# One kernel, one change: the TensorE program of the linear attention becomes a hardware loop over pairs of chunks

## The chip, the cores and the metric

The kernel runs on one core of one Trainium2 chip. The metric is device microseconds per execution of the whole program. It is written by hand in Bass: each engine has its own instruction queue, and every dependency between queues is a semaphore wait.

## The reference

A "macaron" layer over 4 sequences of 1,024 tokens with 128 features, in float32: half of a gated ternary FFN, then a block of causal linear attention with 16 heads of 64 and a GELU MLP, then the same half FFN again. What the change touches is the attention:

```python
Q = _phi((x @ Wq).reshape(b, t, H, DH)).transpose(0, 2, 1, 3)   # _phi = elu + 1
K = _phi((x @ Wk).reshape(b, t, H, DH)).transpose(0, 2, 1, 3)
V = (x @ Wv).reshape(b, t, H, DV).transpose(0, 2, 1, 3)
KV = jnp.einsum('bhti,bhtj->bhtij', K, V)
S = jnp.cumsum(KV, axis=2)
z = jnp.cumsum(K, axis=2)
num = jnp.einsum('bhti,bhtij->bhtj', Q, S)
den = jnp.maximum(jnp.einsum('bhti,bhti->bht', Q, z), EPS_DEN)[..., None]
out = (num / den).transpose(0, 2, 1, 3).reshape(b, t, H * DV)
return out @ Wo
```

## The kernel before

The program has five stages: first FFN, attention, MLP, second FFN, with the ends of the stages overlapped. Large products are made of float32r parts: a high and a low part of the data times a high part of the weights, and the high part times the low weights, so three matmuls each.

The attention goes over 32 chunks of 128 tokens, `n = 0..31`. Two chunks make a half tile `hh` (256 tokens, 16 of them), four chunks make a tile `i` of 512 tokens, and eight chunks make a sequence. For each chunk the TensorE queue does, in this order (`attention_pe`, one Python loop written out in full):

- `token_major("K", n, h)`: the key product of the next chunk, 2 x 3 matmuls of 512 columns (L822, the helper `three`).
- `outputs(g)`: for chunk g = n - 1 first the products of the queries with the running states (L886, steps `I`), then those of the masked scores with the values (L898, steps `O`). They are 64 x 64 tiles; in float32 each of them is two matmul instructions.
- `queries(hh + 1, j)`: the query product of the next half tile, two of its four parts in each chunk (L822, 256 columns), alternating with `token_major("V", n, h)` (L822, 512 columns).
- `transposed_keys(n)` and `transposed_outputs(g)`: transposes (L648).
- `state_products(n)` (L913, steps `D`) and `scores(n)` (L869, steps `S`): again 64 x 64 tiles.
- in every odd chunk the output projection `WO` (24 matmuls of 256 columns, L822) and the transposes of the normalised rows `nT` of the half tile after next.

The queries have two buffers `qf`, the normalised input two pairs `ahh`/`ahl`. ScalarE computes exp and relu of K and Q (L1158, L1159), copies V, the transposed keys and the outputs (L1180, L1188, L1228); VectorE combines exp and relu (L1472, `phi`), divides (L1533 to L1538), takes the low part of the outputs (L1562), adds up the states (L1554) and masks the scores (L1526). GpSimd computes reciprocal roots and the residual sum, SyncE loads and stores. PSUM banks 0, 1, 6 and 7 are a ring; banks 2 to 5 belong to outputs and state products.

A sequence's first chunk leaves out the products with the empty state, its last chunk the state product for the second half of the chunk.

The TensorE program exists twice, as `program(2)` and `program(3)` under a branch on a flag computed on the chip (`pe.If`, `pe.Else`); the first of them is what runs here. Except for this branch no engine jumps anywhere.

Of the kernel before, what the change touches and what calls it, by code (L numbers as in the profile page):

```python
# [5 lines left out]
P = 128  # L6
ALU = mybir.AluOpType
ACT = mybir.ActivationFunctionType
F32 = mybir.dt.float32
# [103 lines left out]
def build_kernel(nc, t, out):  # L113
# [37 lines left out]
    with ctx:  # L151
# [65 lines left out]
        with ExitStack() as s:  # L217
            ahh = [sb(s, f"ahh{h}", [P, 2, P + DH], F32R) for h in range(2)]
            ahl = [sb(s, f"ahl{h}", [P, 2, P + DH], F32R) for h in range(2)]
            ahf = sb(s, "ahf", [P, 2, P + DH])  # L220
            axn = sb(s, "axn", [P, Q, D])
# [5 lines left out]
            ayf = sb(s, "ayf", [P, TILE])  # L227
# [3 lines left out]
            qf = [sb(s, "qf0", [P, PR, TILE // 2])]  # L231
            kt_ = [sb(s, f"kt{k}", [P, DA]) for k in range(2)]
            qf.append(sb(s, "qf1", [P, PR, TILE // 2]))
# [64 lines left out]
        for name, names in (("pe_fn", ["T"]), ("pe_f1", [f"{m}" for m in range(KT)]), ("pe_f2", ["y"]), ("pe_fy", ["T"]),  # L298
# [3 lines left out]
            T[name] = Count(sem(name), names)  # L302

# [46 lines left out]
        def attention_plan():  # L350
# [3 lines left out]
            pe, act, dve, pool, phis, jobs, turns = [], [], [], [], [], [], []  # L354
# [20 lines left out]
            def phi(bank, name):  # L375
                phis.append(name)
                job(bank, name, "act", f"r_{name}")
                act.extend([f"e_{name}", f"r_{name}"])

# [9 lines left out]
            def scores(banks, n):  # L389
                for bank, m in zip(banks, "ab"):  # L390
                    job(bank, f"S{n}{m}", "dve", f"am{n}{m}")

            def state_products(n):
                last = n % CB == CB - 1
                for j in range(2):
                    pe.append(f"D{n}.{j}")
                    jobs.append((f"D{n}.{j}", OB[j], "dve", f"sm{n}.{j}"))
                    if not last:
                        jobs.append((f"D{n}.{j}'", OB[j] + 1, "dve", f"ss{n}.{j}"))
                for name in ("sm",) if last else ("sm", "ss"):  # L400
                    dve.extend(f"{name}{n}.{j}" for j in range(2))
                dve.extend(f"am{n}{m}" for m in "ab")

            def stats(i):
                dve.extend([f"st{i}", f"ag{i}", f"ve{i}"])
                pool.append(f"r1_{i}")

            def once(i):
                dve.extend([f"v1_{i}", f"v2_{i}", f"v3_{i}", f"xp{i}"])
                pool.append(f"r2_{i}")  # L410

            stats(0)
            once(0)
            dve.append("xn0")
            for hh in range(2):
                norm(6 + hh, hh)
                split(hh)
            for h in range(2):
                phi(h, f"K0.{h}")
            dve.append("vt")  # L420
            for j in range(4):
                phi(j, f"Q0.{j}")
            dve.extend([*(f"phi_K0.{h}" for h in range(2)), *(f"phi_Q0.{j}" for j in range(4))])
            for h in range(2):
                values(4 + h, 0, h)
            kt((0, 1), 0)
            state_products(0)
            scores((6, 7), 0)
            stats(1)
            for g in range(NC):  # L430
                c, i, n, hh, old = g % Q, g // Q, g + 1, g // 2, g % CB
                more, queries = n < NC, hh + 1 < NHALF
                if more:
                    for h in range(2):
                        phi(turn(), f"K{n}.{h}")
                        dve.append(f"phi_K{n}.{h}")
                else:
                    for m in range(2):
                        tail((1, 0)[m], f"L0.{m}", "act_f1", f"hi{m}", 0)
# [6 lines left out]
                if c == 1 and i + 1 < NT:  # L446
                    dve.append(f"xn{i + 1}")
                for j in range(2):
                    if queries:
                        phi(turn(), f"Q{hh + 1}.{2 * (g % 2) + j}")  # L450
                        dve.append(f"phi_Q{hh + 1}.{2 * (g % 2) + j}")
                    if more:
                        values(turn(), n, j)
                    if c == 0 and i and j == 0:
                        job(turn(), f"yT{i - 1}", "dve", f"y{i - 1}")
                        dve.append(f"y{i - 1}")
                        pool.append(f"ys{i - 1}")
                if n + 1 == NC:
                    tail(turn(), "N0", "act_fn", "hi", 0)
                if more:  # L460
                    kt((turn(), turn()), n)
                else:
                    for m in range(2):
                        tail((6, 7)[m], f"L0.{m + 2}", "act_f1", ("full2", "hi3")[m], 0)
                    for m in range(2):
                        tail((1, 0)[m], f"L1.{m}", "act_f1", f"hi{m}", 1)
                for j in range(2):
                    job(turn() if more else (2, 5)[j], f"OT{g}.{j}", "dve", f"ol{g}.{j}")
                    act.append(f"oh{g}.{j}")
                    dve.append(f"ol{g}.{j}")  # L470
                if n + 1 == NC:
                    tail(turn(), "N1", "act_fn", "hi", 1)
# [1353 lines left out]
```

## Time and profile before

| what | value |
|---|---|
| median of 3 runs | 854.55 us |
| the runs | 852.06 to 859.12 us |
| profiled execution, its own time | 862.1 us |
| its span, first to last instruction | 860.4 us |
| mean granted TensorE clock | 0.992 |

The profile is one execution. "PE" are TensorE's matmuls, "PEld" its weight loads, which overlap the matmuls; each matmul has one weight load, so that two instructions pass through the queue for each matmul shown. "issue" is time in which an engine waited for nothing that the profile shows. DMA queues q8 and q14 are of the kind "instruction": they bring the engines' program code.

### The profile page before, as it was taken

The page shows a single profiled execution, that of the slowest core. Times are in us where ns is not written, and L with a number is a line of the kernel's source. Part 1 is how long each engine was busy: PE and PEld are TensorE (multiplying, and loading weights), DVE is VectorE, ACT ScalarE, POOL GpSimd, SP SyncE. Part 2 cuts the span into 40 slices and gives each one's busy share as a digit, 9 for nine tenths or more (in the row PEclk, how much of TensorE's full clock was granted, in tenths as well). Part 3 has the DMA queues.
Part 4 walks back from the last instruction along what each step waited for, and adds up shares of the span by engine and source line. Part 5 has one row for each costly group of instructions (what it writes and reads, how often), then busy time and mean ns, then how long its engine had stood idle before and what let it go on. Part 6 is the DMA issues. An engine that isn't in the chain of part 4 may idle for free.

```text
span 860.4 us, 26994 instructions
## 1 busy us (share of the span) xinstructions
PE 796.8 (93%) x11458; PEld 674.6 (78%) x11458; DVE 569.7 (66%) x1290; ACT 563.4 (65%) x1024; POOL 364.4 (42%) x292
## 2 busy tenths in 40 slices
PE   1799999998999999999999999999998799999997
PEld 0688888877788888888888788888786678888886
DVE  7665565376867787687787876778798582818220
ACT  3687777767565654646556556565677477777774
POOL 4597979682001001010000101001276497979784
PEclk9999999999999999999999999999999899999999
DMA  7002120201001001010010100201024320201010
GB/s 256 0 26 60 39 66 8 84 3 51 15 3 41 14 3 53 3 42 14 3 52 4 51 3 27 64 3 40 28 65 118 89 61 13 62 12 50 1 50 26
DMA packets 56762, 34.55 MB, mean 40 GB/s; under 512 B 1984, under 2 KB 55232, under 8 KB 56640
## 3 DMA queue, kind: packets, MB, share of 16 engines
q1 hardware_dynamic: 56640, 32.79, 13.2%
q8 instruction: 93, 1.52, 0.8%
q14 instruction: 29, 0.24, 0.1%
HBM read 22.29 MB, written 10.49 MB: 38 GB/s over the span
## 4 chain that ended last, share of the span: by engine, by line
PE 81%; ACT 6%; issue 5%; DVE 4%; POOL 2%; DMA 1%; SPq 0%; DVEq 0%; ACTq 0%; POOLq 0%
PE ps L677 34%; PE ps L822 21%; PE ps L648 9%; PE ps L886 4%; PE ps L913 4%; PE ps L869 4%; PE ps L898 4%; PE ps L740 3%; ACT ee L1158 1%; DVE xnA L1285 1%; ACT junk L1085 1%; ACT full L1123 1%; DMA xlnA<-x_scratch 1%; ACT gate L1047 1%; POOL alA L1662 1%
## 5 line engine op out<-in xcount | busy, mean ns | idle before, releaser
L1766 POOL TENSOR_TENSOR as<-as,power 128x4 f32<-128x4 f32 x16 | 16.7, 1045 | 292.6 <-DVE as L1485 247.9
L1158 ACT ACTIVATE ee<-ps 128x512 f32<-128x512 f32 x128 | 77.8, 608 | 95.5 <-PE ps L822 69.6
L1662 POOL TENSOR_TENSOR alA<-full,ahA 128x512 fp32r<-128x512 f32 x74 | 100.5, 1371 | 41.9 <-DVE ahA L1325 35.7
L1317 DVE SCALAR_TENSOR_TENSOR full<-ps,sc,gate 128x512 f32<-128x512 f32 x64 | 46.6, 747 | 104.2 <-PE ps L677 63.9
L677 PE MATMUL ps<-ahA,wh 128*128 128x512 f32 x288 | 113.5, 394 | 1.0 <-POOL alA L1662 1.0
L677 PE MATMUL ps<-ahB,wh 128*128 128x512 f32 x288 | 113.4, 394 | 0.1
L677 PE MATMUL ps<-alA,wh 128*128 128x512 f32 x288 | 112.2, 390 | 0.0
L677 PE MATMUL ps<-alB,wh 128*128 128x512 f32 x288 | 112.2, 390 | 0.0
L1662 POOL TENSOR_TENSOR alB<-full,ahB 128x512 fp32r<-128x512 f32 x76 | 99.1, 1318 | 13.0 <-ACT ahB L1066 7.3
L1065 ACT ACTIVATE full<-ps,sc 128x512 f32<-128x512 f32 x86 | 59.5, 692 | 33.3 <-PE ps L677 23.2
L1159 ACT ACTIVATE rr<-ps 128x512 f32<-128x512 f32 x128 | 78.0, 609 | 0.0
L677 PEld LDWEIGHTS ps<-ahA,wh 128*128 128x128 f32 x288 | 54.1, 188 | 13.2 <-POOL alA L1662 2.3
L677 PEld LDWEIGHTS ps<-ahB,wh 128*128 128x128 f32 x288 | 54.1, 188 | 11.4 <-POOL alB L1662 0.6
L677 PEld LDWEIGHTS ps<-alA,wh 128*128 128x128 f32 x288 | 54.1, 188 | 10.9
L677 PEld LDWEIGHTS ps<-alB,wh 128*128 128x128 f32 x288 | 54.1, 188 | 10.8
L1472 DVE SCALAR_TENSOR_TENSOR qf<-ee,rr 128x512 f32<-128x512 f32 x64 | 49.3, 775 | 19.0 <-ACT rr L1159 18.9
L1562 DVE TENSOR_TENSOR ol<-ps,oh 128x512 fp32r<-128x512 f32 x64 | 41.2, 686 | 31.0 <-ACT oh L1228 31.0
L822 PE MATMUL ps<-wah,ahh 128*128 128x512 f32 x128 | 54.5, 426 | 0.3 <-DVE state L1554 0.3
L1243 ACT COPY ayf<-ps 128x256 f32<-128x256 f32 x16 | 6.0, 374 | 73.5 <-PE ps L822 73.5
L869 PE MATMUL ps<-qf,kf 64*64 64x64 f32 x2048 | 39.3, 221 | 13.6 <-issue 13.6
L822 PE MATMUL ps<-wah,ahl 128*128 128x512 f32 x128 | 51.5, 402 | 0.1
L822 PE MATMUL ps<-wal,ahh 128*128 128x512 f32 x128 | 51.2, 400 | 0.0
(179 smaller groups left out, 2248.1 us busy)
## 6 DMA issues: line engine op xcount, KB each, us to landing
wst<-in_ternary SPq DMA_DIRECT2D x5, 512.0 KB, 8.1
stage<-in_attn SPq DMA_DIRECT2D x4, 512.0 KB, 4.6
xlnA<-x_scratch SPq DMA_DIRECT2D x8, 256.0 KB, 2.8
axr<-x_scratch SPq DMA_DIRECT2D x8, 256.0 KB, 4.2
yx_scratch<-ay SPq DMA_DIRECT2D x8, 256.0 KB, 2.3
xs_scratch<-axs SPq DMA_DIRECT2D x8, 256.0 KB, 3.3
xlnA<-yx_scratch SPq DMA_DIRECT2D x8, 256.0 KB, 2.9
xlnB<-yx_scratch SPq DMA_DIRECT2D x8, 256.0 KB, 3.3
```

The source lines that it names most:

```text
L648: ins = nc.tensor.transpose(dst[:, k * P:(k + 1) * P], src, ident[:, :])
L677: ins = nc.tensor.matmul(b[:, :], w[:, col(k):col(k) + P], x_[:, k, :], start=(k == 0 and j == 0), stop=(k == ks[-1] and j == terms - 1))
L822: ins = nc.tensor.matmul(b, w, m, start=(n == 0), stop=(n == len(parts) - 1))
L869: ins = nc.tensor.matmul(banks[m][place, p * DH:(p + 1) * DH], kf[rows, p, place], qf[half][rows, p, tok:tok + DH], start=True, stop=True)
L886: ins = nc.tensor.matmul(banks[j][m][tok, place[p]], qf[(g // 2) % 2][rows, p, first:first + DH], (middle if half else state[k])[rows, p, ...
L1065: nc.scalar.activation(fullh[k % NH][:, :], src, ACT.Gelu, scale=s_).then_inc(*T[f"act_{h}{U}"].step(f"full{m}"))
L1158: nc.scalar.activation(ee[k][:, :], src[:, :], ACT.Exp).then_inc(*X["act"].step(f"e_{name}"))
L1159: nc.scalar.activation(rr[k][:, :], src[:, :], ACT.Relu).then_inc(*X["act"].step(f"r_{name}"))
L1317: nc.vector.scalar_tensor_tensor(fulll[m][:, :], ps[f["bank"]["L1", U, m, "v", n]][:, :], sc[:, KT + m:KT + m + 1], gate[k % NS][:, :], AL ...
L1472: nc.vector.scalar_tensor_tensor(dst, e_, 1.0, r_, ALU.min, ALU.add)\
L1562: nc.vector.tensor_tensor(ol[:, 4 * j:4 * j + 4, own], ps[X["banks"].bank[f"OT{g}.{j}"]][:, :].rearrange("p (k n) -> p k n", n=P), oh[:, 4 ...
L1662: return nc.gpsimd.tensor_tensor(dst, src, hi.bitcast(F32), ALU.subtract)
```

## The change

The TensorE program of the attention is written as `pair(hh)`, two chunks. `pair(0)` and `last_pair(15)` are written out; pairs 1 to 14 are one hardware loop, `pe.Fori(1, NHALF - 1)`, whose body stands once in the code. Only TensorE's queue has the loop; the other queues stay written out in full. For the body to be the same for every pair:

- a wait inside the loop compares a semaphore with a value computed in a register, loop counter times the steps of one pair plus a constant (`hold`). In `outputs`, `state_products` and `scores` a wait on a constant that always holds is put before it.
- the semaphore counts of the work that recurs with a tile and not with a pair (statistics, reciprocal roots, residual) move to semaphores of their own.
- `qf`, `ahh` and `ahl` become one buffer each.
- all four query products go into the odd chunk of a pair (K, outputs, Q0, Q1, V0, Q2, V1, Q3, ...). Normalisation of the next half tile, the output projection of the pair before and its transposes (now per half tile, 2 instead of 4 at once) go into the even chunk.
- a sequence's first chunk computes the products with a state of zeros (a memset in place of a sum on VectorE), its last chunk the state product that was left out.

The core of the diff:

```diff
@@ waits on the TensorE queue
+            rolled, small = [], []
+            def hold(sem, value, per):
+                if rolled:
+                    value = pe.to_reg(rolled[0] * per + (value - per))
+                    if small:
+                        pe.wait_ge(X["pe"].sem, X["pe"].base)
+                pe.wait_ge(sem, value)
+            def after(eng, name):
+                hold(*X[eng].done(name, 0), X["pair"][eng])
             def bank(name):
-                X["banks"].wait_empty(pe, name, 0)
+                if name in X["banks"].prior:
+                    steps, by, _ = X["banks"].prior[name]
+                    hold(*steps.done(by, 0), sum(X["pair"][e] for e in ENG if steps is X[e]))
                 return ps[X["banks"].bank[name]]
@@ outputs
-                        for half, tok in halves if old else halves[1:]:
+                        for half, tok in halves:
@@ state_products
-                both = n % CB < CB - 1
+                both = n + 1 < NC
@@ the TensorE queue
+            def pair(hh):
+                e, o = 2 * hh, 2 * hh + 1
+                for h in range(2):
+                    token_major("K", o, h)
+                outputs(e)
+                norm(hh + 1)
+                for h in range(2):
+                    token_major("V", o, h)
+                if hh:
+                    output_projection(hh - 1)
+                transposed_keys(o)
+                if hh:
+                    back(hh - 1)
+                transposed_outputs(e)
+                state_products(o)
+                scores(o)
+                for h in range(2):
+                    token_major("K", o + 1, h)
+                outputs(o)
+                queries(hh + 1, 0)
+                queries(hh + 1, 1)
+                token_major("V", o + 1, 0)
+                queries(hh + 1, 2)
+                token_major("V", o + 1, 1)
+                queries(hh + 1, 3)
+                transposed_keys(o + 1)
+                transposed_outputs(o)
+                state_products(o + 1)
+                scores(o + 1)
...
+                pair(0)
+                with pe.Fori(1, NHALF - 1) as i:
+                    rolled.append(i)
+                    pair(1)
+                    rolled.pop()
+                X["pe"].next += (NHALF - 3) * X["pair"]["pe"]
+                last_pair(NHALF - 1)
@@ VectorE, phi
-                    if n >= 2 and j == 0:
-                        after("pe", f"O{2 * n - 3}.1")
+                    if n and j == 0:
+                        after("pe", f"I{2 * n - 1}.1")
@@ VectorE, accumulated
-                        if half or old:
+                        if half and n % CB == CB - 1:
+                            ins = nc.vector.memset(after_[:, pairs, :], 0.0)
+                        else:
                             ins = nc.vector.tensor_tensor(after_[:, pairs, :], src, before_[:, pairs, :], ALU.add)
-                        else:
-                            ins = nc.vector.tensor_copy(after_[:, pairs, :], src)
```

## Rows read from the trace of the kernel before

**Rows 1.** The page: busy time by engine, instruction queues, share of the chain that ended last
```profile
PE 796.8 (93%) x11458; PEld 674.6 (78%) x11458; DVE 569.7 (66%) x1290; ACT 563.4 (65%) x1024; POOL 364.4 (42%) x292
...
q8 instruction: 93, 1.52, 0.8%
...
PE 81%; ACT 6%; issue 5%; DVE 4%; POOL 2%; DMA 1%; SPq 0%; DVEq 0%; ACTq 0%; POOLq 0%
```

**Rows 2.** Windows: the attention; busy us and count by engine, granted clock, DMA share, GB/s
```profile
205.00:617.00 412.00, 389.40 (x9491) 344.89 (x9489) 313.71 (x768) 243.37 (x491) 27.05 (x25) 0.99 0.09 26
```

**Rows 3.** Waits of PE, 230 to 617 us: total us, times, longest us
```profile
PE ps L869 <- issue: 13.6, 9, 2.0
PE ps L648 <- DVE xnA L1285: 1.8, 1, 1.8
PE ps L822 <- DVE ol L1562: 1.5, 1, 1.5
PE ps L822 <- DVE state L1554: 1.2, 1, 1.2
PE ps L886 <- issue: 1.1, 2, 0.5
```

**Rows 4.** The chain in order of time around one issue stall: start us, us, what
```profile
258.35 1.09 PE ps L913 x64
259.44 0.48 PE ps L869 x30
259.92 1.52 issue
261.44 0.69 PE ps L869 x29
```

**Rows 5.** DMA of 256 to 261.5 us, 40 slices of 0.1375 us
```profile
GB/s 0 0 0 0 60 0 0 0 0 0 0 0 0 0 0 0 0 0 0 119 0 0 0 0 0 0 0 0 0 0 0 0 0 0 0 0 0 0 0 0
...
q8 instruction: 1, 0.02, 1.5%
```

**Rows 6.** TensorE's timeline, state products and scores without a stall between them
```profile
247.10 1.16 PE L913 MATMUL ps<-vt,kt 64*64 64x65 f32 x64
248.08 1.11 PE L869 MATMUL ps<-qf,kf 64*64 64x64 f32 x64
249.12 0.50 PE L822 MATMUL ps<-wah,ahh 128*128 128x512 f32 x1
```

**Rows 7.** The program's end: last PE matmuls; DMA of 859.9 to 861 us (slices 0.0275 us)
```profile
855.51 0.63 PE L648 MATMUL ps<-ident,yfB 128*128 128x128 f32 x4 [0.88 <-DVE xoA L1291]
...
GB/s 0 0 0 0 0 0 0 0 596 0 0 0 0 0 0 0 0 0 0 0 0 0 0 0 0 0 0 0 0 0 0 0 0 0 0 0 0 0 0 0
```

**Rows 8.** DMA of 856.4 to 858 us, 40 slices of 0.04 us
```profile
GB/s 269 294 307 282 269 691 256 294 256 256 294 269 282 282 282 282 269 282 256 218 141 52 26 0 0 0 0 0 0 0 0 0 0 0 26 102 218 282 282 320
...
q8 instruction: 1, 0.02, 4.6%
```

**Rows 9.** The chain: two long stalls and the key product after each, then an undisturbed one
```profile
325.90 2.00 issue
...
328.86 2.77 PE ps L822 x6
...
380.64 1.88 issue
...
382.86 1.59 PE ps L822 x6
...
343.90 1.40 PE ps L822 x6
```

**Rows 10.** Windows of key product plus outputs: undisturbed, after the stalls of 325.9 and 482.3 us
```profile
238.60:242.30 3.70, 3.70 (x138) 3.09 (x136) 2.00 (x4) 3.13 (x7) 0.00 (x0) 1.00 0.02 4
...
328.80:333.65 4.85, 4.85 (x136) 3.83 (x135) 4.18 (x13) 2.17 (x4) 1.04 (x1) 0.73 0.16 46
...
484.80:490.00 5.20, 5.20 (x139) 4.09 (x135) 4.42 (x13) 2.17 (x4) 1.04 (x1) 0.67 0.21 55
```

**Rows 11.** Lines of VectorE, 205 to 617 us: the shortest instruction and the query combination
```profile
L1472 DVE SCALAR_TENSOR_TENSOR qf<-ee,rr 128x512 f32<-128x512 f32 x64 | 49.3, 775 | 19.0 <-ACT rr L1159 18.9
...
L1481 DVE MEMSET spare<- 128x1 f32 x7 | 0.4, 59 | 0.0
```

**Rows 12.** ScalarE's timeline: exp, relu and a value copy that follow one another
```profile
244.32 0.60 ACT L1180 COPY vt<-ps 128x512 f32<-128x512 f32 x1
244.78 0.63 ACT L1158 ACTIVATE ee<-ps 128x512 f32<-128x512 f32 x1
245.27 0.63 ACT L1159 ACTIVATE rr<-ps 128x512 f32<-128x512 f32 x1
245.75 0.65 ACT L1180 COPY vt<-ps 128x512 f32<-128x512 f32 x1
```

More of the change, by code:

```diff
@@ L387, in kt, with outputs @@
                     act.append(f"kf{n}.{j}")
[L389 to L436, printed above, removed]
-                else:
-                    for m in range(2):
-                        tail((1, 0)[m], f"L0.{m}", "act_f1", f"hi{m}", 0)
+            def outputs(g):
                 pe.extend(f"I{g}.{j}" for j in range(2))
@@ L445, in attention_plan, with transposed @@
                     dve.extend([f"dm{g}.{j}", f"rd{g}.{j}", f"on{g}.{j}"])
-                if c == 1 and i + 1 < NT:
-                    dve.append(f"xn{i + 1}")
+            def transposed(banks, g):
                 for j in range(2):
[L449 to L468, printed above, removed]
+                    job(banks[j], f"OT{g}.{j}", "dve", f"ol{g}.{j}")
@@ L496, in attention_plan @@
             X["banks"] = Banks([(j, b, e if type(e) is Made else X[e], by) for j, b, e, by in jobs], False)
+            X["pair"] = {e: pairs[2][e] - pairs[1][e] for e in ENG}
+            assert all(pairs[k + 1][e] - pairs[k][e] == X["pair"][e] for e in ENG for k in range(1, NHALF - 1))
             return X
@@ L826, in norm @@
             def norm(hh):
-                after("dve", f"xn{hh // 2}")
-                transposes(bank(f"nT{hh}"), [axn[:, q, :] for q in (2 * (hh % 2), 2 * (hh % 2) + 1)], X["pe"], f"nT{hh}")
+                hold(*T["dve_ah"].done("xn", hh), 1)
+                transposes(bank(f"nT{hh}"), [axn[:, q, :] for q in range(2)], X["pe"], f"nT{hh}")
             def token_major(kind, n, h):
-                half, own = (n // 2) % 2, slice(h * DH, h * DH + P)
-                lh, ll = ahh[half][:, n % 2, own], ahl[half][:, n % 2, own]
+                own = slice(h * DH, h * DH + P)
+                lh, ll = ahh[:, n % 2, own], ahl[:, n % 2, own]
                 first = {"K": 1, "V": 2}[kind] * DA + h * TILE
                 cols = slice(first, first + TILE)
+                if kind == "K" and h == 0 and n % 2 == 0:
+                    after("dve", f"hl{n // 2}")
                 three(bank(f"{kind}{n}.{h}")[:, :], [(lh, ll, wah[:, cols], wal[:, cols])], f"{kind}{n}.{h}")
             def queries(hh, j):
-                after("dve", f"hl{hh}")
                 b = bank(f"Q{hh}.{j}")
@@ L1248, in _ @@
+                        continue
+                    for h in range(2):
+                        exp_relu(f"K{o + 1}.{h}")
+                    exp_relu(f"Q{hh + 1}.0")
+                    exp_relu(f"Q{hh + 1}.1")
+                    values(o + 1, 0)
+                    exp_relu(f"Q{hh + 1}.2")
+                    values(o + 1, 1)
+                    exp_relu(f"Q{hh + 1}.3")
+                    transposed_keys(o + 1)
+                    outputs_high(o)
             tern_act(ffn1, attention_first)
@@ L1473, in phi, with row @@
                     .then_inc(*X["dve"].step(f"phi_{name}"))
+            L = T["dve_la"]
+            def row(i, name, ins):
+                ins.then_inc(*L.step(name))
+                wait(dve, "dve_la", name, i)
             def attention_stats(i):
@@ L1740, in ffn_pool @@
                 for t in range(2):
-                    f_rstd(t)
-                for t in range(2):
                     f_norm(t)
```

507 lines of the change are left out of this document (290 added, 217 removed).

## The prediction

> **What bounds the kernel now.** I read the page first, then the windows of the attention, then TensorE's waits, then the stretches around its longest waits. The page says that TensorE is busy 93% of the span and makes 81% of the chain that ended last [rows 1]; in the attention it is busy 389.4 of 412 us [rows 2]. So whatever TensorE does longer or later there lengthens the program almost one for one, and whatever the other engines do shorter brings little. Of TensorE's idle time in the attention the waits on data are few, 1.8, 1.5 and 1.2 us; most is "issue": 13.6 us in 9 stalls ahead of or inside the scores, up to 2.0 us, and 1.1 us elsewhere [rows 3].
>
> These stalls are program code that comes late. In one of them the engine has run the state products and 30 score matmuls, 64 x 64 tiles at 17 ns each, then stands 1.52 us [rows 4]. In the same time one 16 KB packet of queue q8 moves, in the 20th slice of 0.1375 us, at 258.6 us [rows 5], and the engine goes on at 261.44: 2.8 us from the packet's start to its use. q8 is TensorE's: 93 packets [rows 1] for 2 x 11,458 instructions is 246 instructions each, and waits fill the rest of 256. State products and scores together are 128 matmuls, 256 instructions, in 2.0 us when undisturbed (247.10 to 249.12) [rows 6]: a block is used up faster than the next one comes. Had several blocks been loaded ahead, a burst of one block couldn't stall. So the engine holds the block that it runs and the next, and asks for one more when it enters a new block.
>
> **What a jump costs.** The trace has one: after its last matmuls, at 855.51 us [rows 7], TensorE jumps over `program(3)`. A q8 packet shows at 856.60 (sixth slice of 0.04 us) [rows 8], another at 860.12 (ninth slice of 0.0275 us) [rows 7]: target block, then, once the engine runs again, its successor: 3.5 us apart. A jump out of the two blocks so costs between 2.8 us (packet to use) and 4.6 us (855.51 to 860.12). I take 3.6, near the distance of the two packets.
>
> **The change, part by part.** (a) *The back edge.* A pair is 9,491 / 16 = 593 matmuls [rows 2], so 1,190 instructions, nearly five blocks, before the waits' own. At the end of the body the loop's first block is long overwritten, if the engine holds only two. Pairs 1 to 14 make 13 jumps back. When the sequencer reaches the jump, some scores still lie in the engine's queue; they cover between nothing and 1.0 us (a chunk's scores, [rows 6]). I take 0.3: 13 x 3.3 = 42.9 us; bounds 13 x 1.8 = 23 and 13 x 4.6 = 60.
>
> The Trainium skill, "Runtime: NRT & Kernel Launch", section "Instruction fetch mechanics", says that a taken branch whose target isn't among the two pages held forces a fetch before execution goes on; the end of this trace agrees, with its 3.5 us. "Advanced Engine Details and Errata", section "Control Flow Timing", gives about 108 ns for a compare-and-branch; by that alone the back edges would cost 13 x 0.108 = 1.4 us, an estimate.
>
> (b) *The clock.* After the stall of 2.00 us the six key matmuls took 2.77 us where they take 1.40, after that of 1.88 us 1.59 [rows 9]. The windows show the granted clock at 0.73 and 0.67 of full, so partly at 1.2 GHz, and key product plus outputs in 4.85 and 5.20 us instead of 3.70 [rows 10]. A back edge idles longer than any of these stalls. Price 1.15 to 1.5, I take 1.2: 13 x 1.2 = 15.6; bounds 0 and 20.
>
> (c) *The block after the target.* It is asked for only when the engine runs again and is needed after the rest of the first block: the key product (1.4 us, at half clock 2.8) and then outputs at 120 instructions per us. Where the body begins in its block can't be read here: nothing if at the front, up to 3.6 us if at the end. I take 0.6: 7.8 us; bounds 0 and 47.
>
> (d) *Stalls inside the body.* The bursts stay (outputs, state products with scores, 256 instructions each). The 14.7 us of stalls by chance become stalls at places that repeat in all 14 iterations. Taken as equal: 0; bounds -15 and +20.
>
> (e) *Waits against registers.* A body has some 58 such waits, 25 of them in the small-tile stretches, where each has a constant wait too. I count register arithmetic of one or two instructions per wait. Before has neither row; nearest is the shortest instruction there is, 59 ns [rows 11]. In the stretches of large matmuls the work queued ahead (0.23 us per matmul of 512 columns) hides them: nothing. In the small ones 25 x 4 x 0.059 = 5.9 us per pair at most, if nothing covers it, 83 us in all; the queue filled beforehand can cover up to 1.0 us in each of four stretches. Taken as 1.0 per pair, nearer to the covered end because the sequencer keeps up with 8 ns per instruction today: 14; bounds 0 and 83.
>
> (f) *Extra products.* Four sequences' first chunks and three last chunks get 32 more small matmuls each: 7 x 32 x 17 ns = 3.8 us.
>
> (g) *The moves.* The output projection no longer stands right behind the scores, so its waits on low outputs and state (1.5 + 1.2, [rows 3]) go: -3. The odd chunk now holds six exp/relu pairs on ScalarE: instructions there follow every 0.48 us [rows 12], so 12 + 2 + 2 + 2 = 18 of them take 8.7 us, against TensorE's 11.5 (keys and outputs 3.7 [rows 10], queries some 2.8, values 1.4, transposes 1.6, state products and scores 2.0). VectorE is busy 313.7 / 32 = 9.8 us per chunk [rows 2], 3.1 of it four combinations of 0.78 [rows 11]; with six it is 11.3, and its last work ends after TensorE's; what is late there is the masked scores, which the next pair's outputs need 2.5 us after the scores, and the back edge in between covers that. Nothing; bounds -6 and +7. Queued behind TensorE's waits in the odd chunk are only its own later products. The halved transposes, the zeroed state, the new semaphores of GpSimd and SyncE and the single `ahh`, `ahl` lie beside TensorE's work: the copies of `ahh` follow the last value product of the even chunk, half a pair before the keys need them. Nothing.
>
> Sum: 42.9 + 15.6 + 7.8 + 0 + 14 + 3.8 - 3 = 81 us. The profiled execution (862.1 us, span 860.4) is 7.6 above the median 854.55; on its own time 943, on the median 936.
>
> **The rivals.**
> *The body is held on the chip* (faster): TensorE keeps all blocks it has run and only prefetches one ahead. Then 14 iterations fetch nothing, the 14.7 us of stalls and the waits of (g) go, and there is left (f), branches of next to nothing and 5 us of waits: -14.7 - 3 + 3.8 + 5 = -9, 845 us. It decides if the body's six blocks all fit. For it: no row shows a jump back. Against it: whoever has room for six blocks would have loaded more than one ahead, and the stalls of [rows 3] wouldn't be. The Trainium skill, same page and section as above, speaks for it with 128 KiB of instruction memory on TensorE, 2,048 instructions, and against it with a FIFO that holds two pages. Chance 0.09.
> *Cheap back edges*: the queue covers 1.0 us, the fetch takes 2.8, the clock stays: 23 + 14 + 3.8 - 3 = +38, 892 us. For it: the stall of 1.88 us left the clock alone. Chance 0.12.
> *The sequencer becomes the bound*: every register wait of the small stretches counts in full: +69 on top, 1,005 us. Decides when arithmetic costs over some 60 ns. For it: the small stretches run at 8 ns per instruction, with little behind. Chance 0.11.
> Forecast: 0.68.
>
> **The numbers.** 936 us. The range 880 to 990 takes in the cheap edges and the bounds of (a) to (e) as far as they don't all fall on one side, and leaves out the held body and most of the last rival. A difference of 1% is about what can be told from none. Faster by more than that is only the held body with its waits covered, 0.06; within 1% its rest and the lucky tail of the cheap edges, 0.05; slower 0.89.
>
> **What would show it.** Right: in the profile after, one issue stall of about 3 us every 28 to 31 us at the loop's head, ahead of the key product, a fall of the granted clock behind it, 13 times; more q8 packets than 93, since each iteration fetches its five to six blocks and its target anew: some 110. The held body would show some 20 packets and no issue stall in the loop. The sequencer as bound would show short issue idle before every part of L886, L898, L913 and L869, and matmul pitches over 17 ns. Wrong would be the forecast if the stalls at the loop's head are under 2 us or the clock row stays at 9.

## The result, and the profile after

The kernel after takes 859.42 us (median of 8 runs, 857.94 to 862.11); the kernel before, timed beside it, 854.90 us (8 runs, 852.06 to 860.68). The ratio is 1.0053, with 95% of it between 1.0028 and 1.0079: half a per cent slower, within the 1% that the prediction takes as no difference. The forecast was 936 us and its range 880 to 990, so the forecast failed by 77 us and the range didn't hold the time.

The page of the profiled execution (858.43 us) answers to [rows 1]. Columns of the second line: engine, busy time, share of the span, instructions.

```profile
span 856.6 us, 28172 instructions
PE 800.9 (93%) x11682; PEld 677.0 (79%) x11682; DVE 563.5 (66%) x1305; ACT 568.5 (66%) x1024; POOL 367.2 (43%) x292
...
q8 instruction: 31, 0.51, 0.3%
...
PE 65%; ACT 13%; DVE 11%; issue 6%; POOL 4%; DMA 1%; SPq 0%; DVEq 0%; ACTq 0%; POOLq 0%
```

The line to look at is that of q8, TensorE's program code: 31 packets where before had 93. The DMA of the loop's stretch, 270 to 590 us, has no line for q8 at all (columns: packets, MB, share of 16 engines):

```profile
q1 hardware_dynamic: 15840, 7.87, 8.8%
q14 instruction: 9, 0.07, 0.1%
```

The same stretch of before has `q8 instruction: 59, 0.97, 1.3%`. Twelve of the thirteen jumps back lie in this stretch, and not one block is fetched in it. The last packet of TensorE's code before that moves at 260.1 us, at the end of the loop's first turn, and the next at 597.1, behind the loop. One turn, counted in the trace, has 1,312 TensorE instructions: 620 matmuls, 620 weight loads, and 72 for additions in registers, waits and the jump. TensorE's waits of 230 to 600 us, against [rows 3] (columns: us in all, times, longest):

```profile
PE ps L647 <- ACT rr L1209: 4.8, 15, 0.4
PE ps L836 <- DVE ol L1627: 1.2, 1, 1.2
PE ps L884 <- issue: 0.7, 1, 0.7
PE ps L915 <- issue: 0.4, 1, 0.4
```

The stalls on code, 14.7 us before, are 1.1 us, and both are in the first turn (246.9 and 251.2 us), whose code is still being fetched. New is the first row: once per pair TensorE's transposes wait some 0.3 us for ScalarE's relu. The window answers to [rows 2] (columns: stretch, its length, then busy time and count of PE, PEld, DVE, ACT, POOL, the granted clock as a share of full speed, DMA share, GB/s):

```profile
205.00:617.00 412.00, 400.13 (x9851) 352.86 (x9849) 315.46 (x805) 251.53 (x499) 33.19 (x27) 1.00 0.08 23
```

TensorE is busy 400.1 of 412 us, where it was 389.4, and the clock granted is the full 2.4 GHz. So the engine idles less than before and yet isn't done sooner. The chain of one turn of the loop shows why (columns: start, us, what). L903 are the products with the state, L915 the rest of the outputs, L933 the state products, L884 the scores, L836 the large products; the jump back lies between the last scores and the six key matmuls after them.

```profile
390.38 1.09 PE ps L903 x64
391.48 1.14 PE ps L915 x64
...
400.31 1.16 PE ps L884 x64
401.48 1.59 PE ps L836 x6
403.07 1.09 PE ps L903 x64
...
410.20 0.66 ACT ee L1208
410.86 0.50 ACT rr L1209
...
412.06 1.09 PE ps L933 x64
413.15 1.14 PE ps L884 x64
414.28 0.03 issue
414.31 1.65 PE ps L836 x6
415.96 1.07 PE ps L903 x61
```

An undisturbed pair of before, in the same view:

```profile
449.25 1.09 PE ps L886 x64
450.34 0.93 PE ps L898 x64
...
457.19 0.93 PE ps L869 x64
...
473.50 1.09 PE ps L886 x64
```

From one group of products with the state (L886, L903) to the second next, a pair took 473.50 - 449.25 = 24.25 us and now takes 415.96 - 390.38 = 25.58. At the jump back the chain shows 0.03 us. What has grown is small and everywhere: 64 output matmuls 1.14 instead of 0.93 us, 64 scores 1.14 to 1.16 instead of 0.93 (a second one of before had 0.95), and ScalarE's 0.66 + 0.50 in the chain.

Below, three numbers describe a kernel: the **floor**, its shortest pair among pairs 1 to 14 (start of one L903 group to the second next), the **excess**, what these 14 pairs took beyond 14 floors (stalls, slow clock, waits on data), and what lies outside of them. Before is used in its second profile (first experiment), whose own time of 854.76 is nearer the median.

| kernel | start | pair 0 | pairs 1-14 | floor | excess | last pair | end | span |
|---|---|---|---|---|---|---|---|---|
| before, first profile | 213.2 | 27.0 | 365.7 | 24.21 | 26.7 | 12.6 | 241.9 | 860.4 |
| before, again | 213.5 | 26.8 | 358.7 | 24.11 | 21.1 | 12.6 | 241.4 | 853.0 |
| after | 211.7 | 23.4 | 360.9 | 25.48 | 4.1 | 15.7 | 245.0 | 856.6 |
| written out (e2) | 211.5 | 23.8 | 371.0 | 24.84 | 23.2 | 17.2 | 244.3 | 867.8 |
| early registers (e4) | 211.6 | 23.8 | 354.2 | 24.85 | 6.3 | 15.7 | 244.7 | 850.0 |
| e4, tail and query (e7) | 212.5 | 23.2 | 351.7 | 24.60 | 7.3 | 15.7 | 241.2 | 844.3 |

A run's time is longer than its span, by 1.5 to 1.8 us in before, after, e2, e3, e8, e9, e10 and e12, but by 3.2 to 3.8 us in e4 to e7 and in e11. Why isn't shown. Against after, the spans of e4 and e7 therefore look some 1.7 us better than their times, and kernels are compared by times below.

So from before to after the excess of the pairs fell by 17 us, and the floor rose by 1.4 us a pair, 19 us in all. Pair 0 gained 3.4 us and the last pair lost 3.1 (the output projection now comes one pair later), the start gained 1.9, and the end lost 3.6.

The kernels below were timed in three groups (e1 to e4, e5 to e8, e9 to e12), each on one chip with before beside them, and after by itself with before. Before's medians are 854.90 beside after, and 856.77, 857.57 and 856.70 us in the groups. Between kernels of two groups a difference is therefore given twice, from the medians and from the ratios to before.

### The profile page after: what moved, and what is told of

The parts are those of the page before. It is cut to its first block, busy times and chain, and to the rows that moved or that the text cites. A ratio compares the mean times of both kernels' runs of the same rounds, so it can differ in the third digit from the quotient of the medians.

```text
span 856.6 us, 28172 instructions
## 1 busy us (share of the span) xinstructions
PE 800.9 (93%) x11682; PEld 677.0 (79%) x11682; DVE 563.5 (66%) x1305; ACT 568.5 (66%) x1024; POOL 367.2 (43%) x292
## 4 chain that ended last, share of the span: by engine, by line
PE 65%; ACT 13%; DVE 11%; issue 6%; POOL 4%; DMA 1%; SPq 0%; DVEq 0%; ACTq 0%; POOLq 0%
PE ps L676 33%; PE ps L836 13%; PE ps L647 6%; ACT ee L1208 4%; PE ps L884 3%; PE ps L933 3%; PE ps L915 3%; ACT rr L1209 3%; PE ps L903 3%; POOL alA L1740 1%; DVE kt L1530 1%; PE ps L739 1%; POOL alB L1740 1%; DVE am L1592 1%; ACT full L1172 1%
## 5 line engine op out<-in xcount | busy, mean ns | idle before, releaser
L1842 POOL TENSOR_TENSOR as<-as,power 128x4 f32<-128x4 f32 x16 | 19.0, 1190 | 287.0 <-DVE as L1550 256.9
L1530 DVE SCALAR_TENSOR_TENSOR qf<-ee,rr 128x512 f32<-128x512 f32 x64 | 43.7, 691 | 27.4 <-ACT rr L1209 27.0
L836 PE MATMUL ps<-wah,ahh 128*128 128x512 f32 x128 | 55.0, 430 | 1.8 <-DVE ol L1627 1.2
L1344 DVE SCALAR_TENSOR_TENSOR xnB<-xlnB,bagB,rsB 128x128 f32<-128x128 f32 x48 | 45.8, 1014 | 9.0 <-POOL rsB L1744 5.5
L836 PE MATMUL ps<-wah,ahl 128*128 128x512 f32 x128 | 50.4, 393 | 0.0
L836 PE MATMUL ps<-wal,ahh 128*128 128x512 f32 x128 | 50.3, 393 | 0.0
L1530 DVE SCALAR_TENSOR_TENSOR kt<-ee,rr 128x512 f32<-128x512 f32 x64 | 42.8, 688 | 7.2 <-ACT rr L1209 7.2
```

The costliest lines, as they stand in the source:

```text
L836: ins = nc.tensor.matmul(b, w, m, start=(n == 0), stop=(n == len(parts) - 1))
L1344: ins = nc.vector.scalar_tensor_tensor(xn[u][:, q, :], xln[u][:, q, :], bag[u][:, q, 0:1], rs[u][:, q:q + 1].to_broadcast([P, D]), ALU.sub ...
L1530: nc.vector.scalar_tensor_tensor(dst, e_, 1.0, r_, ALU.min, ALU.add)\
```

## The experiments

**Before once more.** The first profile of before may have been an unlucky one: its own time lay 7.6 us above the median, with two falls of the clock. The same kernel, one more profile.

> The kernel before, unchanged, profiled once more. Its first profile (862.1 us) lies 7 us above the median of its runs (854.9). Theory A (the issue stalls of the state-product and score stretches depend on chance, on how a code block falls and on DMA traffic): this profile is nearer the median, with the issue idle of TensorE in the attention under 10 us in place of 14.7, and fewer falls of the clock. Rival B (the stalls are fixed by the code): the same nine stalls at the same matmuls, 13 to 15 us, and the median is lower for a reason outside the attention.

Measured: 854.76 us. TensorE's waits of 230 to 600 us, the chain at the longest stall, and a window behind it (clock third from the right):

```profile
PE ps L869 <- issue: 10.0, 7, 1.9
...
PE ps L886 <- issue: 0.5, 2, 0.3
...
376.99 1.88 issue
...
379.21 2.36 PE ps L822 x6
...
379.70:383.20 3.50, 3.50 (x69) 2.64 (x71) 3.26 (x11) 2.17 (x4) 1.04 (x1) 0.51 0.03 8
```

The stalls on code are there again, at places of the first profile, 10.5 us in place of 14.7. Two of the nine ahead of scores are missing, of 2.0 and 1.8 us, and behind just these two the clock had fallen. It fell once here, behind a stall of 1.88 us. The first profile has a stall of the same length at the same place, and the clock stayed (380.64 us, [rows 9]). So the stalls belong to the kernel, while some 4 us of them, and which of them costs the clock, belong to the single execution. The expectation lies between: a little over its 10 us, one fall in place of two, and not the same nine stalls. All sums of the prediction that start from 862.1 us start from an execution above the usual.

**e2, the body written out.** Everything else of the change stays: order, buffers, products.

```diff
-                with pe.Fori(1, NHALF - 1) as i:
-                    rolled.append(i)
-                    pair(1)
-                    rolled.pop()
-                X["pe"].next += (NHALF - 3) * X["pair"]["pe"]
+                for hh in range(1, NHALF - 1):
+                    pair(hh)
```

> The changed kernel with pairs 1 to 14 written out, so no hardware loop and no register waits; order, buffers and extra products are those of the change. Theory A (the loop saves the code fetches, 15 us of stalls, and its register waits give most of that back): 91 to 95 code packets return and 10 to 15 us of issue idle with them, while the pitch of an undisturbed pair falls from 25.6 to near 24.3 us; the time is within 1% of the change, ratio to before 1.00 to 1.01. Rival B (the register waits cost nothing, and the new order of work is what costs): the pair's pitch stays at 25.6, stalls come on top, 870 us or more, ratio over 1.015. Rival C (the order brings a gain that only the waits eat): under 850 us.

Measured: 866.75 us, ratio to before 1.0109 [1.0076, 1.0143]. The page and the waits:

```profile
q8 instruction: 95, 1.56, 0.8%
...
PE ps L884 <- issue: 10.2, 9, 1.4
PE ps L647 <- ACT rr L1206: 4.3, 12, 0.4
...
PE ps L915 <- issue: 2.0, 3, 1.1
```

Without the loop the change is slower than with it, by 7.3 us from the medians, 4.8 from the ratios (1.0109 - 1.0053). The packets and the stalls on code (12.2 us) are back; so it is the loop that removed them. And without any register the new order alone costs 1.1%: floor 24.84 us against 24.11 to 24.21, and the wait on `rr` is in it. That is the term the prediction had at -3. The floor was expected near 24.3, and the time lies between the two theories: the register waits cost something, and the order does too.

**e3, two pairs in one turn.** The body has 2 x 1,310 instructions, twice as long; nothing is computed otherwise.

```diff
-                with pe.Fori(1, NHALF - 1) as i:
+                with pe.Fori(1, NHALF - 1, 2) as i:
                     rolled.append(i)
                     pair(1)
+                    pair(2)
                     rolled.pop()
-                X["pe"].next += (NHALF - 3) * X["pair"]["pe"]
+                X["pe"].next += (NHALF - 4) * X["pair"]["pe"]
```

> The loop with a body of two pairs, 7 iterations: about 2,800 instructions in place of 1,400. Theory A (TensorE holds a certain amount of code, more than 1,400 and less than 2,800 instructions): every iteration fetches its body anew, 11 to 12 packets each, about 110 in all, and 6 jumps back each stall some 3.3 us: 20 us of stalls at the loop's head, 10 to 15 us of issue stalls inside, 885 to 900 us. Rival B (it holds more than 2,800 instructions): no fetch inside the loop after its first turn, about 35 packets, 859 us or a little under, as with one pair.

Measured: 914.1 us, ratio 1.0648 [1.0601, 1.0695]. The page's q8, the waits, the chain at one jump back and a window behind it; then a window of the whole loop, and that of after (clock third from the right):

```profile
q8 instruction: 108, 1.77, 0.8%
...
PE ps L836 <- issue: 21.6, 6, 3.8
...
290.83 1.33 issue
292.16 2.92 PE ps L836 x6
...
292.10:297.50 5.40, 5.34 (x98) 4.32 (x102) 1.38 (x2) 2.17 (x4) 0.00 (x0) 0.50 0.03 6
...
235.80:650.80 415.00, 371.29 (x8685) 325.65 (x8686) 280.30 (x694) 218.81 (x436) 25.57 (x21) 0.97 0.08 22
...
235.00:596.00 361.00, 353.39 (x8685) 312.82 (x8687) 275.98 (x694) 218.67 (x436) 25.57 (x21) 1.00 0.08 22
```

This is the kernel that the prediction described. Each jump back stops TensorE for 21.6 / 6 = 3.6 us, and the six key matmuls after this one take 2.92 instead of 1.59 us, at a granted clock of 0.50, which is 1.2 GHz; the engine had stood for over 3 us before. The clock fell behind five of the six jumps (windows of 15 or 16 us around them show 0.79, 0.79, 0.89, 0.77, 0.89 and 1.00). The loop takes 54 us longer than that of after: 21.6 at the jumps, 14.5 in more stalls on code inside the body (15.6 of 230 to 640 us against 1.1), and 17.9 in which the same 8,685 matmuls keep TensorE busy. The last part was underrated, and the time came out above the 885 to 900 us expected. The price of a jump was right, that of the clock too low; what was wrong is that the body of one pair would pay them. A body of 1,312 instructions is held, one of 2,620 isn't.

**e4, registers computed ahead.** The loop's waits are against a register that an addition computes just before. In the 64 x 64 stretches nothing covers this. Here the values for those stretches, and for the first wait behind each, are computed earlier, between large matmuls. The waits themselves stay where they are.

```diff
             def hold(sem, value, per):
+                key = id(sem), value, per
                 if rolled:
-                    value = pe.to_reg(rolled[0] * per + (value - per))
+                    if dry:
+                        if key not in held:
+                            held[key] = pe.to_reg(rolled[0] * per + (value - per))
+                        return
+                    value = held.pop(key) if key in held else pe.to_reg(rolled[0] * per + (value - per))
...
-                for h in range(2):
-                    token_major("K", o + 1, h)
+                token_major("K", o + 1, 0)
+                early(lambda: early_outputs(o), lambda: bank(f"Q{hh + 1}.0"))
+                token_major("K", o + 1, 1)
                 outputs(o)
```

> The loop as changed, but the register values for the waits of the small-tile stretches, and of the first wait behind each stretch, are computed ahead of the stretch, behind a large product or the transposes of the keys. Same waits, same number of register instructions. Theory A (about 0.2 us bubbles behind and inside small-tile stretches come from register arithmetic that no queued work covers): the pitch of a pair falls from 25.75 by 0.5 to 1.0 us, 7 to 14 us in all, ratio to before 0.99 to 1.00. Rival B (the wait instructions and their constant companions cost, not the arithmetic): less than 3 us. Rival C (the odd chunk is bound by ScalarE's banks and so nothing moves): less than 2 us.

Measured: 853.94 us (12 runs), ratio 0.9965 [0.9946, 0.9983], which is 5.5 us less than after from the medians and 7.5 from the ratios. The chain has the outputs (L942) and the key product behind the scores of one pair at

```profile
301.24 0.95 PE ps L942 x62
302.19 0.93 PE ps L863 x6
```

0.95 us, where after had 1.14. The floor falls from 25.48 to 24.85 us, that of the written-out kernel. 14 x (25.48 - 24.84) = 9.0 us lie between the floors of e2 and after, and pairs 1 to 14 of e4 take 6.6 us less (360.9 to 354.2). So it is the register arithmetic that costs, in the main. But e4 doesn't only move it: contrary to what was expected, a turn has 18 instructions fewer as well, with 17 plain additions in place of 43 (28,172 - 27,920 = 252 = 14 x 18 by the pages). Whether earlier or fewer is what helps isn't told apart.

**e5, the statistics ahead of the low outputs.** After's end is 3.6 us longer than before's. VectorE's timeline in after: two low outputs wait 2.02 us for ScalarE, and the statistics of the next normalisation, which wait for nothing, stand behind them.

```profile
620.40 1.29 DVE L1627 TENSOR_TENSOR ol<-ps,oh 128x512 fp32r<-128x512 f32 x2 [2.02 <-ACT oh L1248]
621.61 0.86 DVE L1331 BATCH_NORM_STATS2 bstB<-xlnB 128x6 f32<-128x128 f32 x4
...
624.21 3.17 DVE L1344 SCALAR_TENSOR_TENSOR xnB<-xlnB,bagB,rsB 128x128 f32<-128x128 f32 x4 [1.12 <-POOL rsB L1803]
```

On top of e4, in the last pair alone:

```diff
+                        f_stats(3)
                         for j in range(2):
                             low_outputs(o, j)
-                        f_stats(3)
```

> The loop with the register values computed early, and in VectorE's last pair the statistics of tile 3 (f_stats(3)) ahead of the low parts of the last outputs, where the kernel before had them. Theory A (the 3.5 us that the end from the last outputs on takes longer, 245.0 in place of 241.4 us, come from these statistics standing behind low_outputs, which wait for ScalarE): the end shrinks by 2 to 3.5 us, and the time with it, 851 us. Rival B (it is the output projection that has moved into the last pair): under 0.7 us.

Measured: 850.69 us, ratio 0.9918 [0.9894, 0.9942], 3.3 us less than e4 from the medians, 4.0 from the ratios; the end takes 241.2 us in place of 244.7, as in before. In its timeline the statistics come first, and the wait of the low outputs is shorter:

```profile
612.75 0.86 DVE L1362 BATCH_NORM_STATS2 bstB<-xlnB 128x6 f32<-128x128 f32 x4
...
615.18 1.29 DVE L1658 TENSOR_TENSOR ol<-ps,oh 128x512 fp32r<-128x512 f32 x2 [0.94 <-ACT oh L1279]
```

So the longer end isn't due to the loop; it is a place in VectorE's order.

**e6, one query product ahead of the odd chunk's outputs.** On top of e4 as well. ScalarE then gets its third pair of exp and relu 2 us sooner, and the transposes shouldn't find it late.

```diff
                 token_major("K", o + 1, 1)
-                outputs(o)
                 queries(hh + 1, 0)
+                outputs(o)
                 queries(hh + 1, 1)
...
```

> The loop with the register values computed early, and in the odd chunk the first query product ahead of outputs(o), on ScalarE, VectorE and in the ring as well. Theory A (in the odd chunk ScalarE is the bound: it starts on the six exp/relu pairs late, since TensorE does the outputs first, and the transposes wait 0.3 us for the last relu's bank): those waits, 4.5 us in 17, go, the pitch of a pair falls by 0.3 to 0.6 us, 4 to 8 us in all. Rival B (VectorE is the bound there, with its combinations, divisions and masks in one chain): waits move to other places and the time stays within 2 us.

Measured: 850.61 us, ratio 0.9915 [0.9891, 0.9939], 3.3 us less than e4 from the medians, 4.3 from the ratios. The wait fell by half, from 4.5 us in 17 places to 7 places, and the gain is a little under the 4 to 8 us expected:

```profile
PE ps L649 <- ACT rr L1242: 2.3, 7, 0.3
```

**e7, both.**

> Early register values, the statistics ahead of the low outputs at the end, and the first query product ahead of the outputs. Theory A (the three gains lie at different places): they add, 844 to 848 us, ratio to before 0.985 to 0.99. Rival B (one bound behind all): no more than the better of the two alone.

Measured: 847.79 us (5 runs, 846.94 to 848.00), ratio 0.9881 [0.9855, 0.9907]. It is in the 844 to 848 us expected. Timed beside them it is 2.9 us below e5 and 2.8 below e6, so each of the two edits is worth nearly 3 us beside the other as well: the gains add. Against after it is 11.6 us from the medians, 14.7 from the ratios. This kernel beats both before and after.

**e8, written out and without the extra products.** e2 with the conditions of before on each sequence's first and each last chunk, so that the 7 x 32 small matmuls fall away.

```diff
-                        for half, tok in halves:
+                        for half, tok in halves if old else halves[1:]:
...
-                both = n + 1 < NC
+                both = n % CB < CB - 1
...
```

> The written-out pairs (no loop) with the products that the change added left out again: no products with the zero state in the first chunk of a sequence, no second state product in its last. Theory A (they cost TensorE what their number says, 7 x 32 matmuls of 17 ns): 3 to 4.5 us less than the written-out pairs, ratio to before 1.006. Rival B (they are covered by waits in these chunks): under 1.5 us less.

Measured: 866.08 us, ratio 1.0090 [1.0063, 1.0117], 0.7 us less than e2 from the medians and 1.6 from the ratios, with intervals that overlap. The 3.8 us of the prediction aren't confirmed and aren't excluded: this kernel's stalls on code happened to be longer (12.1 us against 10.2 in one profile), which could hide them.

**e9 and e10, how long a body is held.** After, with 640 or 850 pairs of waits that are always met at the end of the body; each pair is one instruction, so the body has 1,952 or 2,162. Nothing computed changes.

```diff
                     pair(1)
+                    for _ in range(640):
+                        pe.wait_ge(X["pe"].sem, X["pe"].base)
+                        pe.wait_ge(X["act"].sem, X["act"].base)
                     rolled.pop()
```

> The changed kernel with 640 more instructions at the end of the loop body (waits that always hold), so 1,952 in place of 1,312. They cost time of their own, some 640 x 51 ns per pair = 33 us, 450 us in all; only the code packets and the branches are of interest. Theory A (TensorE holds eight blocks of 256 instructions, 2,048): no fetch inside the loop after its first turn, some 35 packets, branches of 0.2 us. Rival B (it holds less, for instance six blocks of which the body of 1,312 just fills all): each turn fetches, 120 packets or more, and each jump back takes 3.5 to 4 us.

> The same with 850 more instructions, 2,162 in the body. Theory A (eight blocks, 2,048 instructions): every turn fetches its nine blocks anew, about 140 packets, and the jumps back take 3.5 to 4 us. Rival B (it holds more than 2,162; the two-pair body of 2,600 was too long): some 36 packets, branches of 0.2 us.

Measured: 1930.12 and 2243.56 us, one run each. The q8 line and the longest wait, of e9 and then of e10, each followed by the same wait with the last turn left out (windows 230 to 1,600 and 230 to 1,900 us):

```profile
q8 instruction: 163, 2.67, 0.6%
...
PE ps L836 <- issue: 1021.0, 14, 73.5
...
PE ps L836 <- issue: 951.4, 13, 73.5
```

```profile
q8 instruction: 164, 2.69, 0.5%
...
PE ps L836 <- issue: 1338.1, 14, 96.1
...
PE ps L836 <- issue: 1245.9, 13, 96.1
```

The last turn ends without a jump back and waits 1,021.0 - 951.4 = 69.6 us for 640 instructions, 0.109 us each, over twice the 0.051 that was assumed for them. The 13 others wait 73.2 us on average, so a jump back adds 3.6 us, as in e3. In e10 it is 92.2 us for 850, 0.108 each, and again 3.6 us a jump. With 163 and 164 packets against 31 both bodies are fetched anew in every turn, some ten packets each time. So the limit lies above 1,312 and below 1,952 instructions, 5.1 and 7.6 blocks of 256. That the shorter of the two would be held, because it has fewer than 2,048 instructions, was wrong as put. But a body of 7.6 blocks that doesn't begin at a block's edge touches up to nine, and the prefetch at its end asks for one more; a store of eight blocks isn't excluded. Where in between the limit lies stays open.

**e11, VectorE's statistics later.** e7, with the chain `once` of the next tile (its variance and scale) behind the odd chunk's divisions instead of ahead of them.

```diff
                     masked(o)
-                    if c == 0 and i + 1 < NT:
-                        once(i + 1)
...
                         divided(o, j)
+                    if c == 0 and i + 1 < NT:
+                        once(i + 1)
```

> e7_tail_and_query, and VectorE's normalisation of the next tile (once, 1.1 us of four instructions and three small ones) stands behind the divisions of the odd chunk and not ahead of its first key combination. Theory A (every second pair VectorE is late with the keys and so with everything up to the queries, and that holds the transposes up): 2 to 5 us less than e7 (847.8). Rival B (the queries' combinations at the end of the odd chunk are what is late, and once pushes them now): no change or slower by 1 to 3 us.

Measured: 850.52 us (12 runs), ratio 0.9923 [0.9896, 0.9950]; 2.7 us more than e7 from the medians, 3.6 from the ratios, close to the 1 to 3 us of its rival theory.

```profile
PE ps L649 <- ACT rr L1242: 5.2, 8, 1.0
```

The wait on `rr` is back, up to 1.0 us. ScalarE's own waits on VectorE's query combinations grow too, from 1.1 us in e7 to 3.2 (260 to 600 us). So a likely path is that the statistics delay these combinations, which free ScalarE's buffers, and that ScalarE then comes late for the transposes; the steps in between weren't tested one by one.

**e12, the output projection where it was.** e7, with the projection of a pair right behind the scores at its end, as in before.

```diff
-                if hh:
-                    output_projection(hh - 1)
                 transposed_keys(o)
...
                 scores(o + 1)
+                output_projection(hh)
```

> e7_tail_and_query with the output projection where it was, behind the scores of the odd chunk. Theory A (moving it into the even chunk brought something: behind the scores it waits for the low parts of the last outputs): 3 to 14 us slower than e7 (847.8), with waits of the projection for L1662-like low outputs of 0.3 to 1 us per pair. Rival B (behind the scores it gives VectorE 2.8 us to get the masks done before the next outputs, as before, and the move is what made the pair longer): 3 us or more faster.

Measured: 848.96 us (10 runs), ratio 0.9914 [0.9885, 0.9942], against 847.79 for e7: slower by 1.2 us from the medians and 2.8 from the ratios, and the intervals overlap. Neither theory came true in full (3 to 14 us slower, 3 or more faster).

```profile
PE ps L863 <- DVE ol L1655: 4.2, 14, 2.1
```

The wait on the low outputs that the move was to remove is there in every pair, but 2.1 of its 4.2 us are one place, and the floors are equal (24.7 and 24.6). Pair 0 grows from 23.2 to 26.1 us and the last one shrinks from 15.7 to 12.9: the move carries 3 us of work from the first pair to the last and gains between 1 and 3 us, which these runs can't tell from nothing.

## Why the prediction was wrong

**The step that failed** is the sentence "So the engine holds the block that it runs and the next, and asks for one more when it enters a new block." Its second half was right and its first didn't follow. That a burst of 256 short instructions stalls shows how far ahead the engine *asks*. It says nothing about how long a block that has been run *stays*. From "one ahead" the text went to "two held", and from there to "at the end of the body the loop's first block is long overwritten". After shows no q8 packet in the loop: the body's six or seven blocks stay. The evidence against the held body was the same inference again ("whoever has room for six blocks would have loaded more than one ahead"), a guess at a designer's reasons in place of a row; no row bore on what is kept, and a chance of 0.09 was far too low for that.

The Trainium skill, "Runtime: NRT & Kernel Launch", section "Instruction fetch mechanics", has a taken branch outside of two pages fetch its target. By that rule the loop would have stalled 13 times; for the body of 1,312 instructions the trace disagrees (0.03 us in the chain at the jump, 31 packets), for those of 1,952 and more it agrees (3.6 us a jump). "Advanced Engine Details and Errata", section "Control Flow Timing", gives about 108 ns for compare and branch. Here the measurement differs: the trace of after records the jump back itself with 0.21 us, of which the chain shows 0.03 us as idle, behind scores still queued.

Term by term:

- **(a) back edge 42.9, (b) clock 15.6, (c) next block 7.8:** 66 us forecast, none measured. Once the body is too long, the first price holds: 3.6 us a jump, 3.3 forecast (e3, e9, e10). The clock's is too low: 1.2 us a jump forecast, between 2.1 (3% of 415 us, over six jumps) and 3.0 (17.9 / 6) in e3. The gap of 77 us is essentially these three.
- **(d) stalls inside the body, 0:** they vanished. 14.7 us before (10.5 in the second profile), 1.1 after, all of it in the first turn. In e3, which fetches in every turn, 15.6 us stay, as the 0 had it. With the slower clock and the waits on data that came with them the pairs' excess fell from 21 to 4 us. (e2 has them all again, so it is the loop.)
- **(e) register waits, 14:** the right mechanism, somewhat smaller. The floor rose by 0.64 us a pair from e2 to after, 9.0 in all, of which e4 took back 6.6 in the pairs by computing registers earlier and with fewer instructions. The body has about 45 such waits with one addition each, not 58 with one or two.
- **(f) extra products, 3.8:** unresolved (e8).
- **(g) the moves, -3:** the sign was wrong. e2 carries the moves and (f) without any loop and is 1.1% slower, 9 us. Two of the places are shown: ScalarE's lateness in the odd chunk (2.9 us, e5 to e7) and VectorE's order at the end (2.8, e6 to e7). The text had counted ScalarE's 8.7 us against TensorE's 11.5 and found room. But a sum over a chunk leaves out *when* the work can start: all four query products came behind the outputs, so their exp and relu had to be done in the last part of the chunk. The end of the program wasn't looked at. The other half of the text, that the projection's move saves its waits, isn't refuted: e12 puts the move at 1.2 or 2.8 us, with intervals that overlap. Some 3.6 us of the order's cost stay open, about the size of (f).
- **The base:** 862.1 us lay 7.6 above the median; e1 had 4.2 us less of stalls and one fall of the clock in place of two.

The rival "The body is held on the chip" named the mechanism and said 845. It took off 14.7 and 3 and added 3.8 and 5. With what the profiles of before (the second) and after show, its sum is: excess -17, register waits +9, the new order's higher floor 14 x (24.84 - 24.11) = +10.2, end +3.6, start, pair 0 and last pair together -2.2: +3.6, the difference of the two spans. Its mechanism was right, its terms (e) and (g) were short. That gain and loss nearly cancel is the result: the loop is worth 5 to 7 us (e2 to after) and the order made for it costs 9, of which 5.7 can be had back without giving up the loop (e7 against e5 and e6).

Of what would show it, "more q8 packets than 93" and "a fall of the granted clock" both fell; "some 20 packets and no issue stall in the loop" came true with 31.

## What to carry to other kernels

How far ahead an engine fetches and how much of its program it keeps are two numbers; stalls in straight code show only the first, and a loop lives by the second, so price a loop with both cases before forecasting. On TensorE a body of about 1,300 instructions ran without any fetch and one of 1,950 did not: keep a loop's body short, and compute the registers that its waits compare with in few instructions and between large matmuls, not among small ones (e4 changed both at once). When products are moved, ask of the engine that works on their results not only whether its sum fits but when its first piece can start, and look at the program's end by itself.

## What the runs showed of the hardware

- TensorE's code: one block of 256 instructions is asked for ahead (stalls up to 2.0 us in bursts of as many 64 x 64 instructions, [rows 4, 6]), yet a body of 1,312 instructions loops without a fetch after its first turn; bodies of 1,952, 2,162 and 2,620 fetch in every turn.
- A jump out of the held code stops the engine for 3.6 us on average (21.6 us in 6 in e3, 3.6 a jump in e9 and e10 too). Behind five of e3's six jumps the granted clock fell; behind the one shown 5.4 us ran at 1.2 GHz (0.50). A jump within the held code, 0.21 us by itself, showed 0.03 us of idle behind 64 queued scores.
- A wait that is already met costs TensorE's sequencer 0.109 us with nothing to cover it (69.6 us for 640 in e9; 92.2 us for 850 in e10). In the loop of after the register waits of a pair, about 45 with an addition each, cost 0.64 us in all (floors of e2 and after).
- The same kernel's stalls on code summed to 14.7 us in one profile and 10.5 in the other, with two falls of the clock and one. A stall of 1.88 us at the same place was followed by a granted clock of 0.51 over 3.5 us in one of them and by none in the other.
